# Transposes that accumulate in the last attention, a full last chunk in the first mixture, and six PSUM banks in the first attention

## The chip, the cores and the metric

The kernel runs on one NeuronCore of a Trainium2 chip. It is one launch that computes twelve sublayers of a decoder for 8 sequences of 256 tokens with 256 features in f32. The metric is the device time of one execution in microseconds (us). Five engines work side by side, each with a queue of its own: TensorE (PE; matmuls, with PEld for its weight loads), VectorE (DVE), ScalarE (ACT), GpSimd (POOL) and SyncE (SP, which issues DMAs). PE writes only to PSUM, which has eight banks of 512 f32 per partition; DVE and ACT copy from there.

## The reference

Every sublayer adds to x a function of the layer norm of x. Three of the twelve matter here.

The first is an attention over the batch; the kernel computes it from sums over the sequence, a softmax over the eight sequences, and a value per sequence that is broadcast to all its tokens.

The third (first mixture of experts) sends each token to 2 of 8 experts with I = 704 hidden features. An expert computes `(silu(x Wg) * (x Wu)) Wd`. 704 is five chunks of 128 and one of 64.

The tenth (L3 attention) has 16 heads of 16 features and a learned score by distance:

```python
att = jnp.einsum('bhid,bhjd->bhij', q, k)
dist = jnp.clip(rng[:, None] - rng[None, :], 0, None)
P = jnp.einsum('hrd,bhjd->bhrj', rel_pos_emb[:, :Tx], k)
pos_score = jnp.take_along_axis(P, dist[None, None, :, :], axis=2)
att = (att + pos_score) * (1.0 / math.sqrt(HD))
```

then the causal mask, a softmax and the sum over values. The fifth sublayer (L1 attention) has the same form without the position score.

## The kernel before

The 2048 tokens are 16 tiles of 128 (partitions are tokens, or features after a transpose). Each sublayer is a Stage with one method per engine (`pe`, `act`, `dve`, `pool`, `sp`), in which that engine's instructions are written in order. `between_stages` makes DVE, ACT, POOL and SP wait until the engines before them have ended their last marked step; PE isn't held there, it waits only for data and for banks.

PSUM banks are dealt out by `Uses`: every filling of a bank is a use, and uses take banks in turn, `count` of them (eight by default). `take` makes PE wait until the bank's last use has been emptied by its reader, in this stage or the one before. Banks 6 and 7 also serve `Norm.pe_zT` (line 404), which transposes the normalised x.

*L0Attention.* One use for `m`, eight for `qz` (one per pair of tiles), eight for `v` (the broadcast values v0 to v7, one per sequence, line 658). DVE reads each v (line 703), adds it to x and computes the norm of x for the next stage in between. The next stage, L0Autocorrelation, has `count=6`; its PE begins with eight spectra of the context (one per sequence, 4 f32 products of 256 columns each; 32 products leave 64 records), which need the context and weights from its `fetch`, and bank 0 for the first.

*L0Mixture.* 39 blocks of 128 rows, each of one expert. Per block PE turns the gathered rows (2 transposes, line 1274), makes gate and up in two halves of 352 columns (`pe_half`), transposes the hidden block in six chunks (`pe_hidden`, line 1291; the sixth has 64 columns) and multiplies the chunks with the down weights (`pe_out`; the sixth has 64 rows). The halves of block j stand between the steps of block j-1: half 0 of j, hidden of j-1, half 1 of j, turn of j+1, out of j-1. ACT copies hidden chunks 0 to 3, DVE chunks 4 and 5 with one instruction each (line 1384). SP loads the expert's weights into a ring of four buffers.

*Attention* (used in L1 and in L3). A unit is one bank pair of scores of one query tile: 8 heads with 128 keys or 4 heads with 256. 48 units, six per sequence. Per unit PE writes the mask by a bf16 matmul (line 1734), adds q k (line 1738), in L3 adds the positions (line 1743), then transposes the exponentials of the unit two before (line 1754), and at every second unit sums the values of a group (line 1769). DVE takes the maximum (line 1828), ACT exponentiates (line 1803), DVE copies the transposed scores (line 1839). A unit's scores can start when the exponentials of the unit two before are done. The position tile is stationary, the identity moves, and the product is added into the bank.

In L3 the positions come back from DRAM by a skewed load, 3 MB a sequence, into two sets of buffers; SP issues a sequence's loads when the last scores of the sequence two before are written.

Of the kernel before, what the change touches and what calls it, by code (L numbers as in the profile page):

```python
# [17 lines left out]
P = 128  # L18
B, T, D = 8, 256, 256
# [17 lines left out]
class Signal:  # L37


    def __init__(self, k, name, engine, unit):  # L40
        self.k, self.name, self.engine, self.unit = k, name, engine, unit
        self.sem = k.ctx.enter_context(k.nc.semaphore(name))
        self.reserved = self.raised = 0
# [175 lines left out]
def products(nc, out, pairs):  # L219
    for n, (lhsT, rhs) in enumerate(pairs):  # L220
        last = nc.tensor.matmul(out, lhsT, rhs, start=(n == 0), stop=(n == len(pairs) - 1))  # L221
    return last
# [19 lines left out]
class Moments:  # L242
# [7 lines left out]
    def dve(self, g):  # L250
        k, nc = self.k, self.k.nc
        for i in range(4 * g, 4 * g + 4):
            stats = nc.vector.bn_stats(k.stats[:, i, :], self.src[:, i, :])  # L253
        k.dve.step(stats)
        for i in range(4 * g, 4 * g + 4):
            mean = nc.vector.bn_aggr(self.out[:, i, 0:2], k.stats[:, i, :])  # L256
        mean.then_inc(self.found.up(), 1)
# [358 lines left out]
class L0Attention(Stage):  # L616


    def __init__(self, k):
        self.k, small = k, k.small  # L620
        self.wq, self.wk, self.wvT, self.m = (small[:, P * n:P * n + P] for n in range(4))
        self.s = small[:, 512:768].rearrange("p (i h) -> p i h", i=TILES)
        self.sumT, self.top = small[:, 768:784], small[:, 800:832]
        self.prod = k.slab[0].rearrange("p (i c) -> p i c", i=TILES)
        self.tmp = k.slab[1][:, 0:1024].rearrange("p (n a h e) -> p n a h e", n=2, a=2, h=H)
        self.fetch = Fetch(k, (self.wq, k.d["L0_attn_Wq"]), (self.wk, k.d["L0_attn_Wk"]), (self.wvT, k.d["L0_attn_WvT"]))
        self.norm = Norm(k)
        u = self.uses = Uses(k)
        self.m_use = u.add("dve")
        self.qz = [u.add("dve") for _ in range(TILES // 2)]  # L630
        self.v = [u.add("dve") for _ in range(B)]
        u.close()
        self.summed = k.counter("context_summed", "dve").reserve(1)
        self.shifted = k.counter("logits_shifted", "dve").reserve(1)
        self.exps = k.counter("logits_exp", "act").reserve(1)
        self.added = k.counter("x_added", "dve").reserve(B)
# [34 lines left out]

    def dve(self):
        k, nc, dve, use = self.k, self.k.nc, self.k.dve, self.uses
        dve.wait_ge(*use.filled(self.m_use))
        nc.vector.tensor_copy(self.m, use.bank(self.m_use)[:, 0:P]).then_inc(use.empties(self.m_use), 1)
# [44 lines left out]
class L0Autocorrelation(Stage):  # L720
# [141 lines left out]

    def dve(self):
        k, nc, dve, use = self.k, self.k.nc, self.k.dve, self.uses
        self.taken_out("dve")
        flat, per_head = "p b n -> p (b n)", "p (r e) -> p r e"
# [86 lines left out]
class Router:  # L953
# [71 lines left out]

    def dve(self):
        k, nc, dve, use = self.k, self.k.nc, self.k.dve, self.uses
        self.norm.dve_zT(GROUPS - 1)
        scratch, lg, hot = self.scratch, self.logits, self.hot
# [185 lines left out]
class L0Mixture(Mixture):  # L1215
# [46 lines left out]
        self.ring = [k.loads(f"expert_weights{n}", len(range(n, BLOCKS, self.RING))) for n in range(self.RING)]  # L1262
        self.rows_shared(1, BLOCKS, self.ROWS)

    def rows_of(self, m):
        return min(P, self.I - P * m)

    def pe_turn(self, j):
        k, nc, use = self.k, self.k.nc, self.uses
# [14 lines left out]
    def pe_hidden(self, j):  # L1284
        k, nc, use = self.k, self.k.nc, self.uses
        k.pe.wait_ge(*use.emptied(self.gu[j][-1]))
        for n, u in enumerate(self.hid_use[j]):
            bank = use.take(u)
            for m in range(4 * n, min(4 * n + 4, self.MT)):
                at, M = P * (m % 4), self.rows_of(m)  # L1290
                t = nc.tensor.transpose(bank[0:M, at:at + P], self.hid[j % 2][:, P * m:P * m + M], k.ident)
            t.then_inc(use.fills(u), 1)

    def pe_out(self, j):
        k, nc, use = self.k, self.k.nc, self.uses
        for u in self.hid_use[j]:
            k.pe.wait_ge(*use.emptied(u))
        bank = use.take(self.y_use[j])
        products(nc, bank[:, 0:D], [(self.hidT[j % 2][0:self.rows_of(m), m, :], self.down[j % self.RING][0:self.rows_of(m), m, :])
                                    for m in range(self.MT)]).then_inc(use.fills(self.y_use[j]), 1)  # L1300

    def pe(self):
        pe, use = self.k.pe, self.uses
# [66 lines left out]
    def dve(self):  # L1370
        nc, dve, use = self.k.nc, self.k.dve, self.uses
        self.router.dve()
        self.dve_turn(0)
        for j in range(BLOCKS + 1):
            if j < BLOCKS:
                self.dve_half(j, 0)
            if j:
                u = self.hid_use[j - 1][1]
                dve.wait_ge(*use.filled(u))
                if j >= 3:  # L1380
                    dve.wait_ge(*use.filled(self.y_use[j - 3]))
                for m in range(4, self.MT):
                    M, at = self.rows_of(m), P * (m - 4)
                    last = nc.vector.tensor_copy(self.hidT[(j - 1) % 2][0:M, m, :], use.bank(u)[0:M, at:at + P])
                last.then_inc(use.empties(u), 1)
            if j < BLOCKS:
                self.dve_half(j, 1)
                self.dve_turn(j + 1)
        self.dve_combine()
# [276 lines left out]
class Attention:  # L1666
# [60 lines left out]
    def pe_score(self, h):  # L1727
        k, nc, use = self.k, self.k.nc, self.uses
        n, t, keys, chunks = self.groups[h // 2]
        L, u = P * len(keys), self.at_score[h]  # L1730
        bank = use.take(u)
        for s in range(2):
            last_keys = bank[:, 512 * s:512 * s + 512].rearrange("p (h l) -> p h l", l=L)[:, :, L - P:L]
            nc.tensor.matmul(last_keys, k.ident_bf, k.causal.unsqueeze(1).to_broadcast([P, 512 // L, P]), start=True, stop=True,
                             skip_group_check=True)
        for head, s, p, c, at in self.heads(h):
            strip = slice(32 * s, 32 * s + 32)
            mm = nc.tensor.matmul(bank[:, at:at + L], self.q[p][strip, c, P * t:P * t + P],  # L1738
                                  self.kT[strip, c, P * keys[0]:P * keys[0] + L], start=False, stop=True, skip_group_check=True)
        if self.positions is not None:  # L1740
            for head, s, p, c, at in self.heads(h):
                for a in range(len(keys)):
                    mm = nc.tensor.matmul(bank[:, at + P * a:at + P * a + P], self.positions(t, a, head), k.ident, start=False,  # L1743
                                          stop=True, skip_group_check=True)
        mm.then_inc(use.fills(u), 1)

# [1642 lines left out]
def layouts(inputs):  # L3389

    a = {n: np.asarray(v) for n, v in inputs.items()}
# [17 lines left out]
    t, n = np.arange(T)[:, None], np.arange(P)[None, :]  # L3409
# [23 lines left out]

    I = a["L0_ffn_w_gate"].shape[1]
    down = np.zeros((E, -(-I // P) * P, D), f)
    down[:, :I] = a["L0_ffn_w_down"].transpose(0, 2, 1)
    o["L0_ffn_w"] = np.concatenate(
        [a["L0_ffn_w_" + n].transpose(0, 2, 1).reshape(E, DC, P, I).transpose(0, 2, 1, 3).reshape(E, P, DC * I)
         for n in ("gate", "up")] + [down.reshape(E, -1, P, D).transpose(0, 2, 1, 3).reshape(E, P, -1)], 2)
# [68 lines left out]
```

## Time and profile before

| | |
|---|---|
| three runs | 2885.71, 2892.08, 2893.25 us; median 2892.08 |
| the profiled execution | 2892.69 us, span 2891.4 us |
| instructions | 33874 |
| PE busy | 2459.8 us (85%) |
| PEld busy | 1668.8 us (58%) |
| DVE busy | 1218.3 us (42%) |
| ACT busy | 876.3 us (30%) |
| POOL busy | 556.1 us (19%) |
| chain that ended last | PE 48%, DVE 6%, DMA 2% of the span |
| line 1743 on PE | 768 records, busy 100.2 us |

All times inside the execution count from the start of the span. The profile is of one execution. In its timeline a row is a run of like instructions on one engine; its time is how long the run kept the engine busy, ends of matmuls are modelled, and a matmul's end overlaps the next one's start, so what a group costs is the distance to the next group's start.

### The profile page before, as it was taken

What the parts mean: (1) busy time and instruction counts of PE and PEld (TensorE: products, weight loads), DVE (VectorE), ACT (ScalarE), POOL (GpSimd) and SP (SyncE); (2) the same over time, 40 slices, a digit from 0 to 9 for tenths busy, and PEclk for the clock granted to TensorE, in tenths of its full rate; (3) what the DMA queues carried; (4) which work ended last, traced back from release to release, by engine and by line L of the source; (5) the groups of instructions that cost most, each with busy time, mean ns of one, the idle gap of its engine ahead of it and who ended that gap; (6) DMA issues with size and microseconds to landing.
All of it is one profiled execution on the core that took longest, in us unless ns stands there. A gap on an engine that the chain in (4) does not pass through costs nothing.

```text
span 2891.4 us, 33874 instructions
## 1 busy us (share of the span) xinstructions
PE 2459.8 (85%) x13454; PEld 1668.8 (58%) x13454; DVE 1218.3 (42%) x2269; ACT 876.3 (30%) x2374; POOL 556.1 (19%) x552
## 2 busy tenths in 40 slices
PE   3965999949996779787999999699957999877999
PEld 3854666626674555223566657577732788633555
DVE  6363121257687472565333312300045455655220
ACT  1211222223673341563222321122214444313220
POOL 1441222224101011211444310233120100012000
PEclk8976999969898889898999998799977999988999
DMA  4004777730001000200000002233129232100000
GB/s 152 1 5 191 281 295 284 291 123 1 2 2 49 1 1 29 92 1 29 1 1 0 1 0 73 64 106 96 43 90 364 117 130 91 38 26 1 8 8 15
DMA packets 75380, 224.17 MB, mean 78 GB/s; under 512 B 9359, under 2 KB 52758, under 8 KB 65239
## 3 DMA queue, kind: packets, MB, share of 16 engines
q1 hardware_dynamic: 67894, 204.76, 19.5%
q0 software_dynamic: 7328, 17.26, 1.7%
q8 instruction: 106, 1.74, 0.2%
q14 instruction: 52, 0.42, 0.0%
HBM read 178.61 MB, written 45.17 MB: 77 GB/s over the span
## 4 chain that ended last, share of the span: by engine, by line
PE 48%; DVE 6%; DMA 2%; ACT 1%; POOL 1%; issue 1%; SPq 0%; POOLq 0%; DVEq 0%; ACTq 0%
PE psum L221 26%; PE psum L3198 6%; PE psum L1743 3%; PE psum L2241 2%; PE psum L3207 2%; PE psum L2228 2%; PE psum L1738 2%; DMA positions<-arena 2%; PE psum L1754 1%; DVE stats L253 1%; PE psum L1769 1%; DVE arena L2288 1%; PE psum L2458 1%; POOL small L2656 1%; PE psum L404 1%
## 5 line engine op out<-in xcount | busy, mean ns | idle before, releaser
L221 PE MATMUL psum<-arena 128*128 128x256 f32 (+6 forms) x4100 | 1060.6, 414 | 25.9 <-DVE arena L3294 12.9
L221 PEld LDWEIGHTS psum<-arena 128*128 128x128 f32 (+2 forms) x4100 | 717.3, 184 | 325.8 <-issue 160.5
L1828 DVE TENSOR_REDUCE small<-psum 128x4 f32<-128x1024 f32 (+1 forms) x112 | 137.0, 1223 | 157.4 <-PE psum L1743 110.9
L263 POOL TENSOR_SCALAR x_moments<-x_moments 128x4 f32<-128x4 f32 x48 | 12.0, 249 | 954.2 <-DVE x_moments L256 953.7
L3198 PE MATMUL psum<-arena 128*128 128x512 bf16 x768 | 166.4, 379 | 0.0
L1176 POOL DMA_INDIRECT l_out<-arena,slot_tables x79 | 78.7, 996 | 456.0 <-ACT arena L1348 255.5
L1803 ACT ACTIVATE arena<-psum,small 128x128 f32<-128x128 f32 (+1 forms) x384 | 148.9, 417 | 48.0 <-DVE small L1828 48.0
L1367 DVE TENSOR_TENSOR arena<-arena,psum 128x352 f32<-128x352 f32 x78 | 40.7, 521 | 265.5 <-ACT arena L1326 265.5
L1839 DVE COPY arena<-psum 128x512 f32<-128x512 f32 x224 | 143.6, 681 | 1.8 <-PE psum L1754 1.5
L1803 ACT ACTIVATE z<-psum,small 128x128 f32<-128x128 f32 (+1 forms) x256 | 103.8, 426 | 119.2 <-DVE small L1828 119.2
L404 PE MATMUL psum<-ident,z 128*128 128x128 f32 x256 | 47.1, 344 | 108.6 <-DVE z L274 79.9
L1738 PE MATMUL psum<-arena 32*128 32x128 f32 (+1 forms) x1280 | 133.2, 339 | 0.0
L3198 PEld LDWEIGHTS psum<-arena 128*128 128x128 bf16 x768 | 75.2, 98 | 90.5
L2656 POOL TENSOR_TENSOR small<-small,minus_half 128x16 f32<-128x16 f32 x32 | 92.8, 2901 | 179.2 <-DVE small L2570 179.2
L221 PE MATMUL psum<-zT,arena 128*128 128x512 f32 x240 | 115.2, 636 | 7.3 <-DVE zT L234 4.7
L2786 ACT ACTIVATE arena<-psum,small 128x269 f32<-128x269 f32 x128 | 61.5, 485 | 185.1 <-PE psum L221 173.6
L330 ACT ACTIVATE z<-x,x_shift,x_moments 128x256 f32<-128x256 f32 x96 | 52.2, 593 | 213.4 <-POOL x_shift L271 213.3
L1738 PEld LDWEIGHTS psum<-arena 32*128 32x128 f32 x1280 | 93.3, 191 | 38.9 <-issue 35.2
L221 PE MATMUL psum<-arena,zT 128*128 128x8 f32 (+2 forms) x384 | 108.7, 433 | 5.9 <-ACT zT L230 3.2
L404 PEld LDWEIGHTS psum<-ident,z 128*128 128x128 f32 x256 | 39.4, 181 | 118.4 <-DVE z L274 83.0
L1169 POOL DMA_INDIRECT arena<-z_rows,slot_tables x79 | 80.4, 1018 | 104.4 <-DVE slot_tables L1114 77.3
L1743 PE MATMUL psum<-ident,arena 128*128 128x128 f32 x768 | 100.2, 284 | 0.0
(334 smaller groups left out, 3464.3 us busy)
## 6 DMA issues: line engine op xcount, KB each, us to landing
arena<-L_ffn_w_in SPq DMA_DIRECT2D x39, 2176.0 KB, 8.8
arena<-L_ffn_W_in SPq DMA_DIRECT2D x16, 1024.0 KB
positions<-arena SPq DMA_DIRECT2D x16, 1024.0 KB, 6.0
arena<-positions SPq DMA_DIRECT2D x16, 1024.0 KB, 7.8
arena<-l_out SPq DMA_DIRECT2D x16, 512.0 KB, 8.1
positions<-arena SPq DMA_DIRECT2D x16, 512.0 KB, 6.6
arena<-positions SPq DMA_DIRECT2D x16, 512.0 KB, 8.7
l_out<-arena SPq DMA_DIRECT2D x2, 2048.0 KB, 14.0
```

The costliest lines, as they stand in the source:

```text
L221: last = nc.tensor.matmul(out, lhsT, rhs, start=(n == 0), stop=(n == len(pairs) - 1))
L404: t = nc.tensor.transpose(bank[:, P * j:P * j + P], src[:, P * c:P * c + P], k.ident)
L1169: k.nc.gpsimd.indirect_dma_start(out=out, out_offset=None, in_=k.z_rows[:, :], in_offset=bass.IndirectOffsetOnAxis(ap=self.router.token[0: ...
L1176: k.nc.gpsimd.indirect_dma_start(out=dram[:, :], out_offset=bass.IndirectOffsetOnAxis(ap=self.router.choice[0:count, n:n + 1], axis=0), in ...
L1738: mm = nc.tensor.matmul(bank[:, at:at + L], self.q[p][strip, c, P * t:P * t + P], self.kT[strip, c, P * keys[0]:P * keys[0] + L], start=Fa ...
L1743: mm = nc.tensor.matmul(bank[:, at + P * a:at + P * a + P], self.positions(t, a, head), k.ident, start=False, stop=True, skip_group_check= ...
L1803: e = nc.scalar.activation(buf[:, at:at + L], src[:, at:at + L], ACT.Exp, bias=self.minus_top(h)[:, i:i + 1], scale=1.0, accum_out=self.su ...
L1828: nc.vector.reduce_max(self.minus_top(h), use.bank(u).rearrange("p (h l) -> p h l", l=L), AX_X, negate=True).then_inc(self.topped.up(), 1)
L1839: nc.vector.tensor_copy(self.turned[h % 4][:, 512 * s:512 * s + 512], use.bank(u)).then_inc(use.empties(u), 1)
L2656: k.nc.gpsimd.tensor_tensor(inv, inv, k.minus_half, ALU.pow).then_inc(self.inverted.up(), 1)
L2786: nc.scalar.activation(self.hid[e % 2][:, m, span], use.bank(u)[:, 0:self.half], ACT.Gelu, bias=self.b1[:, e, m:m + 1]).then_inc(use.empti ...
L3198: mm = nc.tensor.matmul(bank, self.w1[:, c, P * m:P * m + P], p[:, c, :], start=(c == 0 and n == 0), stop=(c == MT - 1 and n == 2))
```

## The change

Three things. The position product gets `is_transpose=True` (the position tile is still stationary, the identity still moves, the result is still added into the bank). The sixth hidden chunk becomes the last 128 of the 704 features, which overlap the fifth chunk in 64; the host puts the last 64 rows of the down weights at the end of a padded chunk, with zeros ahead of them, and DVE copies chunks 4 and 5 in one instruction. `L0Attention` deals out six banks.

```diff
-        u = self.uses = Uses(k)
+        u = self.uses = Uses(k, count=6)
...
-    def rows_of(self, m):
-        return min(P, self.I - P * m)
+    def features(self, m):
+
+        at = min(P * m, self.I - P)
+        return slice(at, at + P)
...
-                at, M = P * (m % 4), self.rows_of(m)
-                t = nc.tensor.transpose(bank[0:M, at:at + P], self.hid[j % 2][:, P * m:P * m + M], k.ident)
+                at = P * (m % 4)
+                t = nc.tensor.transpose(bank[:, at:at + P], self.hid[j % 2][:, self.features(m)], k.ident)
...
-        products(nc, bank[:, 0:D], [(self.hidT[j % 2][0:self.rows_of(m), m, :], self.down[j % self.RING][0:self.rows_of(m), m, :])
-                                    for m in range(self.MT)]).then_inc(use.fills(self.y_use[j]), 1)
+        products(nc, bank[:, 0:D], [(self.hidT[j % 2][:, m, :], self.down[j % self.RING][:, m, :]) for m in range(self.MT)]).then_inc(use.fills(self.y_use[j]), 1)
...
-                for m in range(4, self.MT):
-                    M, at = self.rows_of(m), P * (m - 4)
-                    last = nc.vector.tensor_copy(self.hidT[(j - 1) % 2][0:M, m, :], use.bank(u)[0:M, at:at + P])
-                last.then_inc(use.empties(u), 1)
+                last = self.MT - 4
+                nc.vector.tensor_copy(self.hidT[(j - 1) % 2][:, 4:self.MT, :],
+                                      use.bank(u)[:, 0:P * last].rearrange("p (m t) -> p m t", m=last)).then_inc(use.empties(u), 1)
...
-                    mm = nc.tensor.matmul(bank[:, at + P * a:at + P * a + P], self.positions(t, a, head), k.ident, start=False,
+                    mm = nc.tensor.matmul(bank[:, at + P * a:at + P * a + P], self.positions(t, a, head), k.ident, is_transpose=True, start=False,
                                           stop=True, skip_group_check=True)
...
-    down[:, :I] = a["L0_ffn_w_down"].transpose(0, 2, 1)
+    whole = I // P * P
+    down[:, :whole] = a["L0_ffn_w_down"].transpose(0, 2, 1)[:, :whole]
+    down[:, down.shape[1] - (I - whole):] = a["L0_ffn_w_down"].transpose(0, 2, 1)[:, whole:]
```

## Rows read from the trace of the kernel before

**Rows 1.** Page, costliest groups: line, tiles, count | busy us, mean ns | idle before.
```profile
L1743 PE MATMUL psum<-ident,arena 128*128 128x128 f32 x768 | 100.2, 284 | 0.0
```
**Rows 2.** Timeline of PE in L3's attention: start us, busy us, engine, line, tiles, count.
```profile
2314.26 0.38 PE L1734 MATMUL psum<-causal 128*128 128x256 bf16 x2
...
2315.63 2.05 PE L1743 MATMUL psum<-ident,arena 128*128 128x128 f32 x16
2317.52 1.04 PE L1754 MATMUL psum<-ident,z 128*128 128x128 f32 x8
2318.39 0.59 PE L1734 MATMUL psum<-causal 128*128 128x512 bf16 x2
...
2343.43 0.38 PE L1734 MATMUL psum<-causal 128*128 128x256 bf16 x2
```
**Rows 3.** Timeline of PE and DVE in the first mixture.
```profile
447.12 2.53 PE L221 MATMUL psum<-arena 128*128 128x352 f32 x8
...
447.60 0.47 DVE L1384 COPY arena<-psum 128x128 f32<-128x128 f32 x2
...
449.71 5.51 PE L221 MATMUL psum<-arena 128*128 128x256 f32 x20
455.06 0.82 PE L1291 MATMUL psum<-ident,arena 128*128 128x128 f32 x6
455.72 2.53 PE L221 MATMUL psum<-arena 128*128 128x352 f32 x8
```
**Rows 4.** Timeline of DVE and PE around the first attention's end and after.
```profile
57.89 0.68 DVE L703 TENSOR_TENSOR arena<-psum,small 128x512 f32<-128x512 f32 x1
...
68.98 16.32 PE L221 MATMUL psum<-fourier,arena 128*128 128x256 f32 x64 [14.09 <-DVE arena L703]
...
73.73 0.69 DVE L234 COPY arena<-psum 128x512 f32<-128x512 f32 x1 [1.69 <-POOL x_shift L271]
...
85.14 13.98 PE L221 MATMUL psum<-arena 128*128 128x256 f32 x64
98.95 13.33 PE L221 MATMUL psum<-fourier,z 128*128 128x256 f32 x61
```
**Rows 5.** Groups of PE by line and shape, whole span: count | busy us, mean ns.
```profile
L1754 PE MATMUL psum<-ident,z 128*128 128x128 f32 x384 | 50.5, 275 | 1.1 <-DVE arena L1839 1.1
...
L221 PE MATMUL psum<-arena 64*128 64x256 f32 x78 | 27.1, 428 | 0.0
```
**Rows 6.** Timeline of PE in L1's attention, from one batch to the next.
```profile
790.17 0.38 PE L1734 MATMUL psum<-causal 128*128 128x256 bf16 x2
...
808.35 0.38 PE L1734 MATMUL psum<-causal 128*128 128x256 bf16 x2
```
**Rows 7.** Timeline of PE at the start of L3's attention.
```profile
2268.06 0.39 PE L1734 MATMUL psum<-causal 128*128 128x256 bf16 x2 [2.21 <-ACT z L1803]
...
2270.39 3.78 PE L1743 MATMUL psum<-ident,arena 128*128 128x128 f32 x16
...
2283.80 1.08 PE L1769 MATMUL psum<-arena 128*32 128x128 f32 x32
```
**Rows 8.** Timeline of PE at the start of L1's attention.
```profile
741.73 1.97 PE L1754 MATMUL psum<-ident,arena 128*128 128x128 f32 x8
743.49 0.63 PE L1734 MATMUL psum<-causal 128*128 128x256 bf16 x2
...
752.29 1.31 PE L1769 MATMUL psum<-arena 128*32 128x128 f32 x32
```
**Rows 9.** Stretches: us, busy us (records) of PE, PEld, DVE, ACT, POOL, PEclk, DMA, GB/s.
```profile
748.00:752.00 4.00, 4.00 (x19) 2.75 (x16) 2.63 (x5) 1.54 (x7) 0.00 (x0) 0.50 0.02 4
...
912.00:916.00 4.00, 1.98 (x4) 0.68 (x4) 1.61 (x3) 0.70 (x2) 0.55 (x1) 1.00 0.00 0
```
**Rows 10.** Timeline of PE's weight loads in the first mixture.
```profile
451.96 0.29 PEld L221 LDWEIGHTS psum<-arena 64*128 64x128 f32 x2 [0.33 <-issue]
```
**Rows 11.** Stretch at the end of the autocorrelation's loads, columns as in rows 9.
```profile
61.00:62.00 1.00, 0.00 (x0) 0.00 (x0) 1.00 (x6) 0.00 (x0) 0.68 (x2) 0.50 0.22 71
```

## The prediction

> **What bounds the kernel now.** I read the page first: TensorE (PE) has most of the chain that ended last. The change touches three stages, so each was then read by itself: groups of instructions by line and shape (how many records one matmul of the program leaves), then the timeline of the stage, where the distance between two starts is the price of a group. A record's own length (284 ns on average in [rows 1]) holds the pipeline's latency and is no price. In the last attention (L3) PE runs without a gap, 29.17 us from 2314.26 to 2343.43 for one batch of six score units [rows 2]. In the first mixture it is closed too, 455.72 - 447.12 = 8.60 us a block [rows 3]. Between the first attention and the autocorrelation PE stands still for 14.09 us and is released by a VectorE (DVE) product [rows 4].
>
> **Part 1: position scores as transposes.** Line 1743 issues 8 products in each of 48 units, 384 in all, and the profile has 768 records [rows 1]: an f32 matmul leaves two. The transposes at line 1754 of the same stage, 8 a unit, 384 in all, leave 384 [rows 5]. Both have a 128x128 stationary tile and move the identity. In steady state 16 position records take 2317.52 - 2315.63 = 1.89 us, 118 ns each, 236 ns a product; 8 transposes take 2318.39 - 2317.52 = 0.87 us, 109 ns each [rows 2]. So a unit should lose 1.89 - 0.87 = 1.02 us, and 48 units 49 us. The trace shows no transpose that adds into a bank. Bounds: two records a product, as today, give 0; one record at today's 118 ns gives 45.3; 109 ns gives 48.8. The nearest row is line 1754's, so I take 109.
>
> The row says 236 against 109 ns, a ratio of 2.2. The Trainium skill (TensorE: Matmul & The Clock Gate, Terms) calls the transpose mode "4× faster for FP32". By it a product would cost 59 ns and this part would give 384 x 0.177 = 68 us gross. The sum goes by the row.
>
> What is late next? Do ScalarE (ACT) and DVE keep up with 29.17 - 6.1 = 23.1 us a batch? The same Attention class runs in L1 without positions, and there the same maxima, exponentials and copies fit into 808.35 - 790.17 = 18.18 us a batch [rows 6]. Eight transposes a unit on top of L1's batch give 18.18 + 48 x 0.109 = 23.4; the 0.3 us between the two ways is 2.4 us over eight batches, kept for the range.
>
> The start of the stage is different. PE waits for the first exponentials until 2268.06, and then its 16 position records take 3.78 us against 2.05 in steady state: half speed; by the first value sums (line 1769) at 2283.80 it is long over [rows 7, 2]. In L1, which has no full matmuls between scores and transposes, it lasts although PE never stops: eight transposes take 743.49 - 741.73 = 1.76 us, a unit (752.29 - 743.49) / 2 = 4.40 us, up to the value sums at 752.29 [rows 8]; the granted clock is 0.50 there, the 1.2 GHz level [rows 9]. After the change L3 has exactly L1's kinds of instruction before its first sums, so I expect units 2, 3 and 4 at low clock, 4.40 + 1.76 = 6.15 us each. Unit 0 still gives 1.02 (its score leads to the first exponentials), unit 1 nothing (the wait hides it). PE restarts at 2267.04 and reaches the first sums at 2267.04 + 18.4 = 2285.4, against 2283.80 now: 1.6 us late, plus 0.3 for sums that begin at low clock. Units 5 to 47 give 43 x 1.016 = 43.7. Net of this part 43.7 - 1.9 = 41.8 us. Were full speed back as soon as now, it would be 47 x 1.016 = 47.7.
>
> On this the Trainium skill (TensorE: Matmul & The Clock Gate, Part 4) says that full clock "doesn't engage" for the transpose mode. The trace agrees for the start of L1. Taken for the whole stage it is rival E.
>
> **Part 2: last chunk 128 wide, in 39 blocks.** The down product of a block has 12 records, 10 with 128 rows and 2 with 64; there are 78 of the latter [rows 5]. From 447.12 to 449.71 lie 8 gate/up records and two transposes (0.22), so the 8 take 2.37; from 449.71 to 455.06 lie the 12 and another 8, 5.35 in all; the 12 take 2.98 [rows 3]. In a long run of 128-row records of the same 256 columns one takes (98.95 - 85.14) / 64 = 0.216 us [rows 4], so 12 should take 2.59. The weight load of the 64-row pair stands behind an issue gap of 0.33 us [rows 10], and so does the first one after it; a uniform run has none. Gain 0.39 x 39 = 15.2 us. Bounds: 0, if the gap isn't the row count's, and 15.2. I take all, since every other chunk of the same product goes without it. The last transpose gets 128 columns instead of 64: today's six take 455.72 - 455.06 = 0.66 us [rows 3], 110 ns each, already the full-width pitch of [rows 2]; price 0, at most 0.03 x 39 = 1.2 us. The two DVE copies, 0.47 us together [rows 3], become one of as many columns or a few more; PE does over 2 us of other work before it needs them, so 0 (without that cover half of 0.47 a block, 9 us, either way). The weights' bytes don't change: one load a block into a ring of four, so at 8.2 us a block each has three blocks' time.
>
> **Part 3: six banks in the first attention.** Inside the stage the value broadcasts v6 and v7 reuse v0's and v1's banks; should they wait for DVE, the 14.09 us of PE's idleness behind them hide it, so 0. The effect is in the next stage, whose first spectrum takes bank 0. Today that was v7's, the last one DVE reads, and PE starts at 68.98. With six it was v3's, read from 57.89 for 0.68 us [rows 4]; the banks of v4, v5, v6, v7 and v2 follow at or before the times when the next spectra ask for them. The context and weights are the other wait: the DMA share is 0.22 in the microsecond from 61 [rows 11] and nothing after. So PE can start at 61.4. The first six spectra (48 records) need 48 x 0.216 and the 2.35 us that the low clock costs today (85.14 - 68.98 less 64 x 0.216), and end at 74.1. The seventh takes bank 0 again and needs DVE's copy, which starts at 73.73 as today, held by POOL's scale, and takes 0.69 [rows 4]; so 74.55. Two spectra of 8 records end at 74.55 + 3.45 = 78.0; today they end at 85.14. Gain 7.1 us, and PE is closed from there to the products that DVE waits for. Bounds: 0 (the start stays where it is) and 7.6 (no time between the copy and the seventh).
>
> **Sum.** 41.8 + 15.2 + 7.1 = 64.1 us. The profiled execution took 2892.69 us (span 2891.4), so 2828.6; the median of the runs shown lies 0.6 below it: 2828.
>
> **The rivals.**
> A, the forecast: 2828 (2823 to 2834), chance 0.50.
> B, full speed returns in L3 as early as now: 5.9 us better, 2822, chance 0.26. For it: it came back before the first sums there. Against: L1's kinds alone took until the sums.
> C, the earlier spectra bring nothing, because another wait or the low clock eats them: 2835, chance 0.08. For it: the start hangs on one reader and one landing. Against: both have their time in the rows.
> D, the adding transposes cost what the products cost (two records, or a stall at the bank): 2892 - 22.3 = 2870, chance 0.06. For it: no row has this form. Against: everything but the adding is line 1754's.
> E, slower: the clock stays low through the whole L3 attention, since 16 transposes a unit then stand beside kinds of matmul that didn't raise it in L1. A unit costs 4.40 + 1.76 + 1.2 (half of the sums of a group at half speed) = 7.4 us against 4.86 now; 45 units give +114, less 22.3: 2984. It is slower than today once some 18 units run low (64 / 3.55 us each). Against: once risen it stays with little work, for from 912 to 916 PE was busy 1.98 of 4 us at 1.00 [rows 9], and L3 never pauses. Chance 0.05.
> F, an f32 transpose that adds moves at a quarter of a product's time, 59 ns: 19 us better than A, 2809, chance 0.02. No row has a full-width transpose below 109 ns. It is the page's "4×".
> Others, between these: 0.03.
>
> **How the numbers follow.** The low end, 2815, is B with 7 us for terms taken too small; the high end, 2846, takes in C, the 3.5 us of the 118 ns bound, the 2.4 us of the L1 comparison and a third of part 2. D and E are left out. A measurement of this kernel can't tell some 0.3%, 9 us, from no change; A to D and F are beyond it. Faster 0.92, same 0.03, slower 0.05.
>
> **What would show it.** Right: line 1743 with 384 records, eight of them in 0.87 us; a batch of 23.1 to 23.4 us; half speed in L3 until the first line 1769; no 64-row record and 8.2 us a block; PE's first spectrum at 61.4 and the eighth's end at 78. Wrong: 768 records or a pitch over 120 ns; PE idle before line 1734, waiting for ACT's line 1803, in steady state; a granted clock of 0.5 behind the first sums; a block still at 8.6 us; PE idle until 68.98.

## The result, and the profile after

The kernel after takes 2824.02 us (median of 4 runs, 2820.61 to 2827.16) against 2891.79 for the kernel before beside it; the ratio is 0.9769, 95% interval 0.9748 to 0.9790, some 67 to 68 us less. The profiled execution took 2827.16 us (span 2825.9), 65.5 below that of before. Forecast were 2828 in a range of 2815 to 2846.

The page's groups show the first step: the same line, half the records, the same length of one (compare [rows 1]).

```profile
L1743 PE MATMUL psum<-ident,arena 128*128 128x128 f32 x384 | 53.3, 283 | 0.0
```

PE's timeline of L3's attention, the start and a steady batch (start us, busy us, engine, line, tiles, count, idle before and releaser):

```profile
2242.40 1.09 PE L1743 MATMUL psum<-ident,arena 128*128 128x128 f32 x8
2246.67 0.61 PE L1734 MATMUL psum<-causal 128*128 128x256 bf16 x2 [3.17 <-ACT z L1803]
...
2249.22 1.97 PE L1743 MATMUL psum<-ident,arena 128*128 128x128 f32 x8
2250.98 1.46 PE L1754 MATMUL psum<-ident,z 128*128 128x128 f32 x8
2252.27 0.38 PE L1734 MATMUL psum<-causal 128*128 128x256 bf16 x2
...
2253.64 1.09 PE L1743 MATMUL psum<-ident,arena 128*128 128x128 f32 x8
2254.57 1.04 PE L1754 MATMUL psum<-ident,z 128*128 128x128 f32 x8
2255.45 0.38 PE L1734 MATMUL psum<-causal 128*128 128x256 bf16 x2
...
2258.72 1.08 PE L1769 MATMUL psum<-arena 128*32 128x128 f32 x32
...
2260.00 0.38 PE L1734 MATMUL psum<-causal 128*128 128x256 bf16 x2
...
2283.42 0.38 PE L1734 MATMUL psum<-causal 128*128 128x256 bf16 x2
```

Eight adding transposes take 2254.57 - 2253.64 = 0.93 us, the eight plain ones behind them 0.88. The 16 records of before took 1.89 [rows 2]. A batch went from 29.17 us [rows 2] to 2283.42 - 2260.00 = 23.42. There is also the row that goes against the forecast. PE restarts at 2246.67 at half speed, as before [rows 7], but full speed is back during the transposes of 2250.98 (1.29 us to the next group's start, where eight at low clock take 1.76 [rows 8]), two units ahead of the first value sums at 2258.72.

The first mixture, PE's timeline:

```profile
433.09 2.53 PE L221 MATMUL psum<-arena 128*128 128x352 f32 x8
...
435.67 5.12 PE L221 MATMUL psum<-arena 128*128 128x256 f32 x20
440.63 0.82 PE L1293 MATMUL psum<-ident,arena 128*128 128x128 f32 x6
441.29 1.05 PE L221 MATMUL psum<-arena 128*128 128x352 f32 x3
```

The stretch of twelve down and eight gate/up records is 440.63 - 435.67 = 4.96 us instead of 5.35 [rows 3], the block 441.29 - 433.09 = 8.20 instead of 8.60. This stage has no 64-row records left. Six transposes take 0.66 us as before.

Between the first attention and the autocorrelation:

```profile
62.03 16.65 PE L221 MATMUL psum<-fourier,arena 128*128 128x256 f32 x64 [6.81 <-DMA arena<-L_xattn_bo_in]
78.52 13.98 PE L221 MATMUL psum<-arena 128*128 128x256 f32 x64
```

PE starts 7 us earlier than in [rows 4], now released by the last of the loads, and the first spectra end at 78.5, where they ended at 85.1.

The 65.5 us by stretch, from landmarks of the two traces (starts of the named PE records):

| stretch | before | after | gain |
|---|---|---|---|
| start to the autocorrelation's w transpose | 164.3 | 157.7 | 6.6 |
| from there to the mixture's first row transpose | 97.6 | 98.0 | -0.4 |
| mixture, first row transpose to last hidden transpose | 337.2 | 322.3 | 14.9 |
| its combine, to L1's first score transposes | 142.6 | 140.6 | 2.0 |
| L1 and mixture-of-depths attention to the last transpose | 305.2 | 308.6 | -3.4 |
| to L3's first position record | 1213.4 | 1212.7 | 0.7 |
| L3, first to last position record | 232.1 | 186.2 | 45.9 |
| to the last matmul | 394.9 | 395.6 | -0.7 |

The loss of 3.4 us is in stages that the change doesn't touch, and it lies in two places. Record by record, the kernel after is 23.1 us ahead where PE restarts in L1 (716.09 against 739.18), 21.6 once L1's low clock is over, and 19.5 at the first mask of the mixture-of-depths attention (969.87 against 989.39): 1.5 us at L1's start, some 2 behind L1's attention, where the clock had fallen earlier. The same four projections there, before and after:

```profile
919.19 1.95 PE L221 MATMUL psum<-zT,arena 128*128 128x512 f32 x4 [0.72 <-DVE zT L234]
```
```profile
899.01 3.75 PE L221 MATMUL psum<-zT,arena 128*128 128x512 f32 x4 [0.72 <-issue]
```

### The profile page after: what moved, and what is told of

Same layout as the page of the kernel before. It is cut to its first block, busy times and chain, and to the rows that moved or that the text cites. A ratio compares the mean times of both kernels' runs of the same rounds, so it can differ in the third digit from the quotient of the medians.

```text
span 2825.9 us, 33068 instructions
## 1 busy us (share of the span) xinstructions
PE 2400.1 (85%) x13070; PEld 1628.7 (58%) x13070; DVE 1215.5 (43%) x2230; ACT 878.2 (31%) x2374; POOL 558.8 (20%) x552
## 4 chain that ended last, share of the span: by engine, by line
PE 48%; DVE 7%; DMA 2%; ACT 1%; POOL 1%; issue 1%; SPq 0%; POOLq 0%; DVEq 0%; ACTq 0%
PE psum L221 26%; PE psum L3198 6%; PE psum L2241 2%; PE psum L3207 2%; PE psum L2228 2%; PE psum L1738 2%; PE psum L1743 2%; DMA positions<-arena 2%; PE psum L1754 1%; DVE stats L253 1%; PE psum L1769 1%; DVE arena L2288 1%; PE psum L2458 1%; POOL small L2656 1%; PE psum L404 1%
## 5 line engine op out<-in xcount | busy, mean ns | idle before, releaser
L221 PE MATMUL psum<-arena 128*128 128x256 f32 (+6 forms) x4100 | 1045.8, 412 | 26.2 <-DVE arena L3294 13.3
L234 DVE COPY arena<-psum 128x512 f32<-128x512 f32 (+1 forms) x32 | 22.2, 698 | 174.2 <-PE psum L2738 116.9
```

## The experiments

Eleven kernels were made beside a repetition of the kernel after. A change of a few us is lost in the spread of whole runs, so landmarks and the granted clock of the profiles are read as well as the times.

**One part at a time.** Three kernels are the kernel before with one part of the change each.

```diff
# e1: position products only
-                    mm = nc.tensor.matmul(..., self.positions(t, a, head), k.ident, start=False,
+                    mm = nc.tensor.matmul(..., self.positions(t, a, head), k.ident, is_transpose=True, start=False,
# e2: features(), the full last chunk, the one copy and the host's layout only
# e3: L0Attention only
-        u = self.uses = Uses(k)
+        u = self.uses = Uses(k, count=6)
```

> The kernel before with the position products as transposes, nothing else. My theory (an f32 product leaves two records of 118 ns, a transpose one of 109 to 116 ns; nothing else in L3 becomes late): line 1743 has 384 records, a batch of six units takes 23.4 us instead of 29.17, and the kernel is 45 to 48 us faster, about 2846. Rival (part of the 46 us seen in L3 came from elsewhere in the whole change, such as another state of the clock or other times of the DMAs): under 40 us.

2839.16 us against 2885.59 for before beside it, ratio 0.9836 (0.9820 to 0.9853). L3 from first to last position record took 185.5 us, 46.6 less than before; the rest of this profile equals that of before but for some 6 us ahead of L3. A batch:

```profile
2265.22 0.38 PE L1734 MATMUL psum<-causal 128*128 128x256 bf16 x2
...
2288.64 0.38 PE L1734 MATMUL psum<-causal 128*128 128x256 bf16 x2
```

23.42 us, as in the whole change. All of L3's gain belongs to this part.

> The kernel before with the 128-wide last chunk, nothing else. My theory (the 64-row pair of records costs 0.39 us a block more than a full pair): 8.20 us a block instead of 8.60, 15 us faster, about 2877. Rival (the block was also freed by the single copy or by weights that come earlier): a gain that differs from 15 by more than 3 us.

2866.52 us, ratio 0.9927 (0.9907 to 0.9946), 19 to 21 us less and so more than the 15 expected. In the profile the mixture gave 14.9 us, from 337.2 to 322.3, exactly as in the whole change. Of the rest of this profile's gain, 5.2 us lie between the second mixture's last transpose and L3's first position record (193.5 us, where the profile of before has 198.7); e1's and e3's profiles have 194.0 and 193.7 there, so it was the profile of before that was long, not this kernel that is short. The block was not freed by anything else. Why the times gave more than 15 us isn't shown: e2's four runs lie at 2859.8, 2862.9, 2870.2 and 2871.1.

> The kernel before with six banks in the first attention, nothing else. My theory (the first spectrum waits for the last reader of bank 0): it starts at 62 instead of 69, released by the loads, and the kernel is 6.5 to 7 us faster, about 2885. Rival (a wait later in the autocorrelation takes it back): no more than 2 us.

2878.28 us, ratio 0.9978 (0.9969 to 0.9988), 6 to 7 us less. PE starts its spectra at 60.82 after 6.46 us of idleness (before: 14.09, [rows 4]); the w transpose comes 8.6 us earlier, 1.6 of which were there already at the v broadcasts (47.6 against 49.2). Nothing takes it back later. PE's row names DVE's reader and not the loads:

```profile
60.82 15.77 PE L221 MATMUL psum<-fourier,arena 128*128 128x256 f32 x64 [6.46 <-DVE arena L703]
```

The read that ended just ahead of it, at 60.77, is v4's, of bank 1, though. v3's, of bank 0, had ended at 56.97, and the kernel after didn't wait for v4's (it starts at 62.03, that read ends at 62.50). The traffic of the loads ended at 60.0, so they are the likelier releaser here too.

**Is it the row count?** The kernel after, whose last down product reads only 64 rows:

```diff
-        products(..., [(self.hidT[j % 2][:, m, :], self.down[j % self.RING][:, m, :]) for m in range(self.MT)])
+        products(..., [(self.hidT[j % 2][P * self.MT - self.I if m == self.MT - 1 else 0:P, m, :],
+                        self.down[j % self.RING][P * self.MT - self.I if m == self.MT - 1 else 0:P, m, :])
+                       for m in range(self.MT)])
```

> The kernel after, but the down product of the last chunk reads only the 64 rows that aren't zero (partitions 64 to 127); the 128-wide transpose and the single DVE copy stay. My theory (the number of rows of the product costs the time, by weight loads that aren't overlapped): the block is back at 8.6 us, 15 us slower than the kernel after, about 2839. Rival (the one copy instead of two, or the full-width transpose, gave the time): within 3 us of the kernel after, 2824.

2833.23 us where before takes 2885.59, ratio 0.9818 (0.9802 to 0.9835), against 0.9776 (0.9759 to 0.9792) for the repetition of the kernel after: 12 us of 15 by the ratios, and in the trace all of it. The mixture is back at 337.2 us to the tenth, with the wide transposes and the one copy in place. PE's timeline and, last, a weight load:

```profile
440.83 2.53 PE L221 MATMUL psum<-arena 128*128 128x352 f32 x8
...
443.42 5.51 PE L221 MATMUL psum<-arena 128*128 128x256 f32 x20
448.77 0.82 PE L1293 MATMUL psum<-ident,arena 128*128 128x128 f32 x6
449.43 2.53 PE L221 MATMUL psum<-arena 128*128 128x352 f32 x8
```
```profile
445.67 0.29 PEld L221 LDWEIGHTS psum<-arena 64*128 64x128 f32 x2 [0.33 <-issue]
```

5.35 us for the twenty records again, and the issue gap of [rows 10] is back. Whether these rows start at partition 0, as before, or at 64, as here, makes no difference.

**Is it bank 0?**

```diff
-        u = self.uses = Uses(k, count=6)
+        u = self.uses = Uses(k, count=7)
```

> The kernel after, with seven banks instead of six in the first attention. Bank 0 was then v5's, which DVE reads until 63.8, and bank 1 v6's, until 67.6. My theory (the first spectrum waits for the last reader of bank 0, then for the loads): PE starts at 64 instead of 62, released by DVE's line 703 and no more by the loads, and the eight spectra end 1 to 2 us later than with six. Rival (six banks help since 6 and 7 stay with the transposes): the start is as with eight, 69, for bank 6 is again shared.

One run, 2824.19 us. The timeline of DVE and PE:

```profile
61.82 0.68 DVE L703 TENSOR_TENSOR arena<-psum,small 128x512 f32<-128x512 f32 x1
```
```profile
62.65 16.74 PE L221 MATMUL psum<-fourier,arena 128*128 128x256 f32 x64 [7.90 <-DVE arena L703]
79.22 2.97 PE L221 MATMUL psum<-arena 128*128 128x256 f32 x13
```

v5's read ends at 62.50 and PE starts at 62.65. This profile is 1.3 us ahead of the kernel after's before this point (DVE's first read of a v at 50.88 against 52.20), so the start is at 64 on that scale, and the spectra end 2.0 us later than with six banks (79.22 + 1.3 against 78.52). Sharing bank 6 did no harm.

**What does the clock follow?** The step that failed is about this. First the kernel after again:

> The kernel after, once more, as the base for the three fillers that run beside it. By my prediction's step (half speed at an attention's start lasts until the first value sums, since scores and transposes alone don't bring the clock back) its L1 start runs at half speed for about 13 us of PE's work and its L3 start for 18. Rival (the level comes back some time after the pause, whatever the kinds): the lengths differ from profile to profile of one kernel, and L3's is nearer to 5 us, as in the first profile of it. About 2824, or 2818 on a chip where the kernel before takes 2885.

2826.91 us (2819.47 to 2827.23), before 2890.20. A low stretch is the time at a granted clock of 0.50 at an attention's start, where PE pauses for the first exponentials. L3's was 3.4 us, in the kernel after's first profile 6.8; L1's was 17.1 in both. Then three fillers, written by PE into a bank that is free, while it waits for an attention's first exponentials:

```diff
             if h < U:
                 self.pe_score(h)
+            if h == 1:
+                self.keep_busy()
...
+    def keep_busy(self):
+        bank = k.psum[:, 512 * 7:512 * 8]     # after a wait for its last reader
+        # e5: 12 x
+            nc.tensor.matmul(bank, k.ident_bf, k.causal.unsqueeze(1).to_broadcast([P, 4, P]), start=True, stop=True)
+        # e6: 24 x
+            nc.tensor.transpose(bank[:, at:at + P], k.ident, k.ident)
+        # e8: 6 x
+            nc.tensor.matmul(bank[:, 0:256], self.q[0][0:32, 0, 0:P], self.kT[0:32, 0, 0:256], start=True, stop=True)
```

> The kernel after, with 12 full bf16 matmuls of 512 columns (2.6 us, into a bank that is free then) in each attention while PE waits for the first exponentials. My theory (the pause before the third unit drops the clock, and its cost is that low stretch): the clock stays at 1.00 at the start of L1, of the mixture-of-depths' part and of L3; L1 8 us faster, L3 2 us, 10 us in all. Rival (the low level comes from the kinds of instruction that follow, not from the pause): it falls all the same, and the time is that of the kernel after within 3 us.

> The same filler from 24 f32 transposes of 128x128 (2.6 us) instead of matmuls. If transposes don't keep the clock up, as the prediction's step had it, and as the Trainium skill says (TensorE: Matmul & The Clock Gate, Part 4), the granted clock falls as without the filler and the time is the kernel after's. If they count like any work, the clock and the time are those of the filler of matmuls, about 10 us faster.

> The same filler from 6 f32 products with 32 rows and 256 columns (12 records, about 2.6 us), a quarter of the array. If what drops or keeps the low level are the narrow products of the scores, the granted clock falls as without the filler. If PE's being occupied is enough, it stays at 1.00 and the kernel is about 10 us faster than the kernel after.

| kernel | median us | low stretch in L1, mixture of depths, L3 (us) |
|---|---|---|
| after, again | 2826.91 | 17.1, 6.8, 3.4 |
| e5, matmuls | 2812.96 | 0, 0, 0 |
| e6, f32 transposes | 2815.35 | 0, 0, 0 |
| e8, 32-row products | 2823.35 | 17.1, 6.8, 3.4 |

The ratios to before, which takes 2890.20 us beside all four, are 0.9776 (0.9759 to 0.9792), 0.9737 (0.9721 to 0.9753), 0.9747 (0.9731 to 0.9764) and 0.9766 (0.9749 to 0.9783). By the ratios e5 is 11 us and e6 8 us faster than the kernel after, where 10 were expected; e5's interval lies clear of the repetition's, e6's overlaps it a little. Stretches of L1's start: the first of e5 and e6 hold the filler, those of after and e8 what came behind the pause (columns as in [rows 9]; PEclk is the third number from the end). The kernel after, e5, e6, e8:

```profile
716.00:732.00 16.00, 15.91 (x90) 10.91 (x90) 7.99 (x11) 8.64 (x41) 0.00 (x0) 0.50 0.01 1
```
```profile
704.00:710.00 6.00, 4.60 (x36) 2.55 (x36) 1.91 (x2) 5.21 (x24) 0.02 (x1) 1.00 0.01 1
709.00:724.00 15.00, 14.65 (x165) 10.64 (x166) 12.18 (x17) 11.59 (x54) 0.00 (x0) 1.00 0.00 1
```
```profile
709.00:715.00 6.00, 4.67 (x48) 4.06 (x50) 1.99 (x2) 5.12 (x24) 0.00 (x0) 1.00 0.00 1
714.00:724.00 10.00, 9.57 (x98) 6.87 (x98) 7.62 (x11) 8.18 (x40) 0.00 (x0) 1.00 0.01 2
```
```profile
715.00:731.00 16.00, 16.00 (x91) 11.27 (x92) 7.99 (x11) 8.04 (x38) 0.00 (x0) 0.50 0.01 1
```

PE did about the same microseconds of work in the pause each time. Full-array work held the level, and it didn't matter whether it was a matmul or an f32 transpose. Work on 32 rows held nothing. The Trainium skill (TensorE: Matmul & The Clock Gate, Part 4) says that full clock "doesn't engage" for the transpose mode; here e6's row at 1.00 contradicts it for f32 transposes.

Holding is not raising, so the same two kinds were added where PE is busy at half speed, behind the transposes of L1's units 2 to 5:

```diff
+            if 2 <= h < 6 and U == 48 and self.positions is None:
+                self.more_work()      # e9: 8 f32 transposes; e10: 2 products with 32 rows, 256 columns
```

> The kernel after, with 8 more f32 transposes (1.76 us at half clock) behind the scores and transposes of units 2 to 5 of L1's attention, so that its start has the mix that L3's has now. If full-array work, transposes included, is what brings the clock back, and the 32-row products of the scores don't, L1's low stretch becomes as short as L3's, 3.4 to 7 us instead of 13.7 to 17.1. If its length is chance or belongs to L1's place, it stays at 13.7 to 17.1 us.

> The control: the same places filled with two 32-row products of 256 columns (4 records, also about 1.8 us at half clock). If only full-array work counts, L1's low stretch stays at 13.7 to 17.1 us or grows. If it is simply more work between the scores that helps, it is as short as with the transposes.

One run each, beside 2884.92 for before: e9 2814.31 us, e10 2828.47. PE's timeline of e9, then of e10:

```profile
713.47 1.97 PE L1763 MATMUL psum<-ident,arena 128*128 128x128 f32 x8
715.23 1.74 PE L1754 MATMUL psum<-ident 128*128 128x128 f32 x8
716.81 0.38 PE L1734 MATMUL psum<-causal 128*128 128x256 bf16 x2
...
718.18 1.09 PE L1763 MATMUL psum<-ident,arena 128*128 128x128 f32 x8
```
```profile
717.09 1.97 PE L1762 MATMUL psum<-ident,arena 128*128 128x128 f32 x8
718.99 2.07 PE L1753 MATMUL psum<-arena 32*128 32x256 f32 x4
...
729.98 1.97 PE L1762 MATMUL psum<-ident,arena 128*128 128x128 f32 x8
731.88 2.07 PE L1753 MATMUL psum<-arena 32*128 32x256 f32 x4
733.88 1.94 PE L1777 MATMUL psum<-arena 128*32 128x128 f32 x32
```

With eight more transposes full speed is back inside the first filled unit (1.74 us, then everything at full pace); the low stretch is 6.8 us instead of 17.1. From PE's restart to the mask behind the third value sums e9 takes 737.61 - 710.92 = 26.69 us, the kernel after 744.37 - 716.09 = 28.28 for the same units without the extra transposes. One run, without the kernel after beside it, doesn't show that the whole kernel is faster. With the narrow products the low stretch lasts 23.9 us, longer than without. Even the value sums at 733.88 run at half speed (1.94 against 1.08).

**A version beyond both.** The matmul filler, and the last chunk of 42 features in L1's mixture of depths treated as part 2 did:

```diff
-                M, bank = min(P, self.dff - P * m), use.take(u)
+                at, bank = min(P * m, self.dff - P), use.take(u)
...
-                              [(self.hid[0:min(P, self.dff - P * m), m, P * b:P * b + P], self.w3[0:min(P, self.dff - P * m), m, :])
+                              [(self.hid[:, m, P * b:P * b + P], self.w3[:, m, :])
```

> The filler of matmuls and, in L1's mixture of depths, the same treatment of its last chunk of 42 features as the first mixture got: 128 wide, overlapping, zeros in the weights. There are 8 products with two 42-row records each. By what the 64-row pair cost (0.38 us) this gives 3 us more than the filler alone: about 78 to 80 us below the kernel before, some 2810 where that takes 2890. If the cost was peculiar to 64 rows, it is the time of the filler alone.

2807.01 us (5 runs, 2805.42 to 2809.99) against 2884.92 for before, ratio 0.9730 (0.9716 to 0.9743). The intervals of this and of e5 (0.9721 to 0.9753) overlap, so the times don't show the second step, but the traces do: from the first of these matmuls to line 2053 it is 1111.53 - 1048.72 = 62.81 us, in e5 1110.48 - 1043.94 = 66.54. Of these 3.7 us 3.1 lie in the down products (from their first record at 1090.81 it is 20.72 us, in e5 from 1086.63 23.85), for 8 pairs of 42-row records 0.39 each, what the 64-row pair cost. The other 0.6 lies in the gate and up products ahead of them, whose last chunk is wider too and where the granted clock of the first 8 us differs a little (0.84 and 0.82); these two weren't separated. In this profile the clock had fallen ahead of L1's filler, during the narrow scores, and the twelve matmuls took 4.45 us instead of 2.76; full speed was back right behind them. The filler in L1 is no certain remedy.

## Why the prediction was right, and the step that failed

The sum was 64.1 us, measured were 65.5 between the profiled executions. Point by point:

- *The unit loses a record per product and 1.02 us.* Right in mechanism (384 records, e1). The size was 1.89 - 0.93 = 0.96, since eight transposes right behind the narrow scores pay a little, 0.93 where the next eight take 0.88. The comparison with L1's batch had that in it: it gave 23.4 us a batch, measured 23.42; the difference from 23.1 was set aside for the range and should have been in the sum.
- *DVE and ACT keep up.* Right; PE waits for line 1803 only at the start.
- *Half speed in L3 lasts until the first value sums, because scores and transposes alone don't bring the clock back.* This step failed. The forecast took 41.8 us for part 1, and it gave 45.9, near rival B's 47.7 less the 2.4 of the batches. Full speed came back after some 5 us of work, in e1 and the repetition after even less. L1 has the same kinds but half of the transposes, and e9 shows that this is the difference: with as many transposes as L3's, L1's start is as short. I had counted the kinds and left out how much there is of each. This rests on one profile with more transposes and one control (e10); fewer transposes in L3 weren't tried. In L1's low stretch I also took the value sums for the cause of the end, where they only stood beside it: in the kernel after (17.1 us) and in e10 they run at half speed themselves.
- *Part 2 gives 0.39 us in 39 blocks, 15.2.* Right, 14.9, and e4 shows that the row count is the whole of it.
- *Part 3 gives 7.1, by bank 0's last reader.* Right, 6.6; the loads' traffic ended at 61.4 as read from the DMA share, but PE began 0.6 us behind it, at 62.0, a step that the forecast put at nothing. The 0.13 us between the end of DVE's copy (74.42) and the seventh spectrum (74.55) had no row either. e7 moved the start to exactly the reader that its bank count names.
- *Rivals.* D, E and F are out: one record, 0.93 us for eight, full speed behind the start. C is out by e3. B held, with 0.26 given to it and 0.50 to A.

That the sum came out within 1.4 us is luck. The three parts gave 45.9 + 14.9 + 6.6 = 67.4 us, 3.3 more than forecast, and the stages outside them took back 1.8 in these two profiles (3.4 lost at L1's start and behind its attention, part of it gained elsewhere), which no step of mine foresaw.

What stays open: executions of one kernel lie in two groups 6 to 7 us apart (the kernel after 2820.6 and 2821.0, 2827.1 and 2827.2). The profiles of different kernels show such a difference in stages that none of them touches: from the mixture-of-depths attention's last transpose to L3's first position record it is 1213 to 1214 us in before, after, its repetition and e8, 1206 to 1207 in e1 to e4, e9 and e10, and 1209 in e7. It can't be the whole of it: e2's profiled execution (2871.1) is in its slower group and has 1206. No two profiles show both groups of one kernel, so what separates them stays open. Nor is it shown why L1's stretch is 13.7 us in two profiles and 17.1 in the others that leave its start alone.

## What to carry to other kernels

Count the records that a product of the program leaves before pricing it: an f32 product by the identity costs two, the same thing as a transpose one, also when it adds into a bank. Pad a contraction's last chunk to full height by overlapping the one before, with zeros in the weights, when it costs no extra copy. See whose bank the next stage's first product takes, since PE can run ahead of a stage's end. And before an engine pause is accepted as free, look at the clock behind it: a few full-array instructions in the pause can be worth more than the pause.

## What the runs showed of the hardware

- An f32 transpose that adds into PSUM has the pitch of one that doesn't: 0.93 us for eight behind narrow products, as line 1754's have in L1 in the same place (745.74 to 746.67). Plain ones in a run take 109 to 110 ns; a longer run of adding ones is in no trace.
- A pair of records with fewer rows than its neighbours costs 0.39 us more than a full pair (64 rows, at partition 0 or 64, and 42 rows); its weight loads and the next full one each stand behind an issue gap of 0.33 us.
- In L1's start full-array work, f32 transposes included, held TensorE's granted clock at 1.00 (e5, e6) and brought it back sooner (e9, one profile). Being occupied wasn't enough: PE was busy 22.00 of 22.00 us in e10 at 0.50, the 1.2 GHz level, with 32-row products in more than half of that time.

```profile
715.00:737.00 22.00, 22.00 (x103) 14.16 (x104) 8.00 (x11) 8.07 (x38) 0.00 (x0) 0.50 0.00 1
```
